# Routed feed-forward and attention steps: block-wise state signals, operation choice inside the feed, key table by operation, broadcast weight loads, drains on two engines

## What is computed

```
def step(h, p):
    op = jnp.argmax(h[0, 0, :NOPS])          # NOPS = 19
    q, k, v = h @ p['wq'][op], h @ p['wk'][op], h @ p['wv'][op]
    attn = softmax(einsum('bqd,bkd->bqk', q, k) * scale)
    y = einsum('bqk,bkd->bqd', attn, v) @ p['wo'][op]
    h = where(p['am'][op], y, h)
    z = relu(h @ p['w1'][op] + p['b1'][op]) @ p['w2'][op] + p['b2'][op]
    return where(p['fm'][op], z, h)
```

## Time and profile before

| | us |
|---|---|
| Executions timed | 602.72, 610.61, 612.91 |
| Median of the three | 610.61 |
| Profiled execution, its own time | 602.83 |
| Span in its profile | 600.8 |
| Granted TensorE clock over the span | 0.942 of full speed |

### The profile page before, as it was taken

One profiled execution on the slowest core, in us unless ns is written; L12 is line 12 of the kernel. 1 busy time (PEld: TensorE's weight loads), 2 busy tenths in 40 slices (PEclk: granted clock), 3 DMA queues, 4 the chain that ended last, 5 costly groups with the idle time before them and its releaser, 6 DMA issues.

```text
span 600.8 us, 10365 instructions
## 1 busy us (share of the span) xinstructions
PE 529.1 (88%) x3951; PEld 255.0 (42%) x3952; DVE 404.9 (67%) x740; ACT 318.4 (53%) x584; POOL 49.8 (8%) x106
## 2 busy tenths in 40 slices
PE   6999998998599989999999999999999652799962
PEld 5554654554133335444334443344444320366721
DVE  5655557357886746876887686876662556898662
ACT  2735445565256575556656566666656332655440
POOL 7031232113110000000000010000000000000000
PEclk9999999699679999999999999999999957999975
DMA  5000000000000000000000000000000000000001
GB/s 112 5 1 2 2 2 2 0 2 2 0 1 1 1 1 1 2 0 1 1 1 1 1 2 1 1 9 1 1 1 1 2 3 15 1 1 1 1 0 35
DMA packets 9511, 3.28 MB, mean 5 GB/s; under 512 B 8820, under 2 KB 9079, under 8 KB 9463
## 3 DMA queue, kind: packets, MB, share of 16 engines
q1 hardware_dynamic: 8182, 2.61, 1.9%
q10 hardware_dynamic: 1281, 0.01, 0.1%
HBM read 2.09 MB, written 0.52 MB: 4 GB/s over the span
## 4 chain that ended last, share of the span: by engine, by line
PE 76%; DVE 10%; issue 8%; ACT 3%; POOL 1%; POOLq 0%; DVEq 0%; ACTq 0%
PE PS L786 18%; PE PS L763 18%; PE PS L747 5%; PE PS L667 4%; PE PS L681 4%; PE PS L694 3%; PE PS L518 2%; PE PS L490 2%; PE PS L502 2%; PE PS L802 2%; PE PS L708 2%; PE PS L989 2%; PE PS L564 2%; DVE most L1550 2%; PE PS L582 1%
## 5 line engine op out<-in xcount | busy, mean ns | idle before, releaser
L1189 ACT ACTIVATE PT<-PS 128x512 f32<-128x512 f32 x256 | 138.7, 593 | 78.7 <-PE PS L763 78.3
L1550 DVE TENSOR_REDUCE most<-PS 128x2 f32<-128x1024 f32 x128 | 154.4, 1221 | 33.9 <-PE PS L747 33.0
L763 PE MATMUL PS<-qrow,aS 128*64 128x512 f16 x1024 | 134.5, 383 | 1.8 <-ACT PT L1189 1.8
L786 PE MATMUL PS<-PT,V 128*64 128x512 f32 x512 | 134.4, 604 | 0.0
L763 PEld LDWEIGHTS PS<-qrow,aS 128*64 128x64 f16 x1024 | 58.8, 110 | 68.8 <-issue 22.9
L1145 ACT ACTIVATE prob<-sbias,negm 128x320 f32<-128x320 f32 (+1 forms) x64 | 34.3, 537 | 44.1 <-DVE negm L1596 43.9
L747 PE MATMUL PS<-aS,qrow 64*128 64x512 f16 x256 | 41.6, 397 | 7.0 <-DVE most L1550 6.2
L786 PEld LDWEIGHTS PS<-PT,V 128*64 128x64 f32 x512 | 32.0, 136 | 37.0 <-ACT PT L1189 17.9
L667 PE MATMUL PS<-ident 128*128 128x256 f16 x128 | 39.1, 306 | 7.5 <-DVE negm L1596 6.3
L1307 POOL TENSOR_TENSOR rstd<-var,minus_half 128x8 f32<-128x8 f32 (+1 forms) x9 | 13.5, 1505 | 343.5 <-DVE var L1414 343.5
L339 DVE COPY PT<-PS 128x384 f32<-128x384 f32 (+1 forms) x32 | 16.7, 523 | 29.4 <-PE PS L694 29.3
(11 more groups left out here) (192 smaller groups left out, 657.2 us busy)
## 6 DMA issues: line engine op xcount, KB each, us to landing
xall<-in_x_dram SPq DMA_DIRECT2D x2, 256.0 KB, 4.4
out_dram<-x SPq DMA_DIRECT2D x4, 128.0 KB, 2.1
w<-in_L_attn_Wq_dram SPq DMA_DIRECT2D x2, 128.0 KB, 2.6
w<-in_L_attn_Wk_dram SPq DMA_DIRECT2D x2, 128.0 KB, 2.7
w<-in_L_attn_Wv_dram SPq DMA_DIRECT2D x2, 128.0 KB, 2.7
fc<-in_L_conv_fc_w_dram SPq DMA_DIRECT2D x2, 64.0 KB, 2.7
wu<-in_L_attn_Wu_dram SPq DMA_DIRECT2D x2, 64.0 KB, 2.3
w1s<-in_L_ffn_ffn_w_dram SPq DMA_DIRECT2D x2, 64.0 KB, 2.1
```

The source lines that it names most:

```text
L763: mm = pe.matmul(PS[h0:h0 + C, lane, :], aS[:, part, k0 + h0:k0 + h0 + C], qG[:, lane, toks], start=(part == 0), stop=(part == 1))
L786: mm = pe.matmul(PS[cols, 6 + g % 2, :], V[:, img * NT + kt, cols], PT[:, g % 2, lane, kt, :], start=(kt == 0), stop=(kt == NT - 1))
L1189: act.activation(PT[:, g % 2, lane, phase, :], PS[:, lane, :], ACT.Exp).then_inc(c1["exped"], 1)
L1550: dve.tensor_reduce(most[:, g % 2, u // 2, u % 2, :], PS[:, b0:b0 + 2, :], AX.X, ALU.max, negate=True)\
```

## The change

- **State by block.** One semaphore per block, `state_made[blk]`, counts how often the block has been written; the registers `nw` and `nb` hold that count now and at the update's begin. Every reader waits for its block's count alone. SP waits for blocks 1 and 3 (`state_read`) before it issues wo in an attention, and before w2s, b1s and b2s in a feed.
- **Order.** Blocks go in the order 0, 2, 1, 3 (`ORDER`), the routed pieces likewise.
- **Choice inside the feed.** PE does hidden 0 to 2, output 0, hidden 3, then `show_row` into bank 3 (`ROW`) as soon as block 0 is drained, then output 1. DVE does `choose` between its last hidden drain and its last output drain. Only an update without a feed chooses afterwards (`otherwise`, in an Else).
- **Key table.** Laid out operation by step; the key is 4 x (19 x step + operation) + flags less NONE, zero if dead, so one instruction and a contiguous reduction replace `keys_left`'s three; the table takes eight steps instead of seven. The word carries the operation: `choose` writes one number, and SP needs no `value_load`.
- **Weights.** ws, w1s and wo come by one DMA each that reads the source twice (128 rows), so that ACT and DVE split them with one instruction instead of two. ACT splits w1s ahead of the state.
- **Drains.** y of lane 0 is drained by ACT, lane 1 by DVE; the last y goes into OB. Feed outputs use banks 2 and 6.
- **Way out.** PE turns each block when its count is there, into banks 4, 5, 2, 3, without waiting for adds.

The core of the diff, with the lines that it adds and keeps; those that it takes out are in the listing above, except where a minus shows them. Indentation is cut by eight.

```diff
@@ scan
+        now_word = e.snap(word, min_val=0, max_val=4 * NOPS * NSTEP - 1)
         flags = e.snap(now_word % 4)
         e.reg_add(nu, nu, 1)
+        e.reg_mov(nb, nw)
         now = e.snap(nu, min_val=1, max_val=NSTEP)
+        with e.If(flags >= 2):
+            attend(e.snap(na, min_val=0, max_val=NSTEP - 1), written(), before(), now_word, now)
+            e.reg_add(na, na, 1)
+            e.reg_add(nw, nw, 1)
+        with e.If(e.snap(flags % 2) == 1):
+            feed(e.snap(nf, min_val=0, max_val=NSTEP - 1), written(), before(), now_word, now)
+            e.reg_add(nf, nf, 1)
+            e.reg_add(nw, nw, 1)
+        if otherwise:
+            with e.Else():
+                otherwise(written(), now)
...
@@ pieces
-ROUTED = [(what, lane, b) for what in ("k", "q") for lane in range(2) for b in range(NB)]
+ROUTED = [(what, lane, b) for what in ("k", "q") for b in range(NB) for lane in range(2)]
...
@@ PE, attend: y
+            if (g, lane) == (0, 0):
+                pe.wait_ge(wo_loaded, base(16) + 16)
+            elif (g, lane) != (1, 1):
+                pe.wait_ge(state_made[0 if g == 0 else 2], nw + 1)
...
@@ PE, feed to the end
+    def feed(nf, nw, nb, word, now):
+        bz, bs = pe.snap(nf * (B * NB)), pe.snap(nf * N_STATE)
+        def hidden_part(j):
+            pe.wait_ge(ffn_split, bs + (2 + j))
             pe.sem_inc(gate, 1)
+            toks = slice(ORDER[j] * BLK, (ORDER[j] + 1) * BLK)
             for half, filled in enumerate(("lo_filled", "hi_filled")):
                 for part in range(2):
+                    m = pe.matmul(PS[:, 2 * j + half, :], w1S[:, part, half * P:(half + 1) * P],
+                                  hS[:, toks], start=(part == 0), stop=(part == 1))
                 m.then_inc(rf[filled], 1)
+        def output_part(two):
+            pe.wait_ge(rf["lo_drained"], bz + 2 * (two + 1))
+            pe.wait_ge(rf["hi_drained"], bz + 2 * (two + 1))
             pe.sem_inc(gate, 1)
             for half in range(2):
                 for n in range(2):
+                    blk = ORDER[2 * two + n]
+                    m = pe.matmul(PS[n * C:(n + 1) * C, (2, 6)[two], :], w2s[:, half, :],
                                   Z[:, half, blk * BLK:(blk + 1) * BLK], start=(half == 0), stop=(half == 1))
             m.then_inc(ffn_out_filled, 1)
+        for j in range(3):
+            hidden_part(j)
+        output_part(0)
+        hidden_part(3)
+        pe.wait_ge(state_made[0], nw + 1)
         pe.sem_inc(gate, 1)
+        show_row()
+        output_part(1)
+    def otherwise(nw, now):
+        pe.wait_ge(state_made[0], nw)
+        pe.sem_inc(gate, 1)
+        show_row()
+    nw = scan(pe, attend, feed, otherwise)
+    for j, blk in enumerate(ORDER):
+        pe.wait_ge(state_made[blk], nw)
+        pe.sem_inc(gate, 1)
+        for k in range(QT):
+            t = blk * QT + k
+            m = pe.transpose(PS[:, (4, 5, 2, 3)[j], k * C:(k + 1) * C], aT[:, t * P:(t + 1) * P], ident[0:C, 0:C])
+        m.then_inc(end_filled, 1)
...
@@ ACT
+    def high_state(made, j, nw):
+        toks = slice(ORDER[j] * BLK, (ORDER[j] + 1) * BLK)
+        act.wait_ge(state_made[ORDER[j]], nw)
+        act.sem_inc(gate, 1)
+        act.activation(hS[0:C, toks], aT[:, toks], ACT.Copy).then_inc(made, 1)
+    def attend(na, nw, nb, word, now):
         base = lambda k: act.snap(na * k)
+        for j in range(2):
+            high_state(routed_high, j, nw)
         act.wait_ge(attn_loaded, base(48) + 48)
+        twice = ws[:, :, :].rearrange("c n (o d) -> c n o d", o=1).to_broadcast([P, 3, 2, C])
+        act.activation(wsS[:, 0], twice, ACT.Copy).then_inc(routed_high, 1)
+        for j in range(2, B * NB):
+            high_state(routed_high, j, nw)
         for n, piece in enumerate(ROUTED):
             act.wait_ge(routed_filled, base(len(ROUTED)) + (n + 1))
             high_part(piece, PS[:, n % 4, :], (1.0, C ** -0.5), routed_high)
+        def y_out(g):
+            act.wait_ge(c2["y_filled"], base(B * NB) + (2 * g + 1))
+            act.activation(aT[:, g * BLK:(g + 1) * BLK], y_bank(g, 0)[0:C, :], ACT.Copy)\
+               .then_inc(state_made[g], 1)
+        act_attention(act, c2, base, 2, y_out)
+    def feed(nf, nw, nb, word, now):
+        bz = act.snap(nf * (B * NB))
+        act.wait_ge(ffn_loaded, act.snap(nf * 64) + 64)
+        act.activation(w1S[:, 0], w1s[:, :], ACT.Copy).then_inc(ffn_high, 1)
+        for j in range(B * NB):
+            high_state(ffn_high, j, nw)
+        def drain_hidden(j):
+            toks = slice(ORDER[j] * BLK, (ORDER[j] + 1) * BLK)
+            act.wait_ge(rf["lo_filled"], bz + (j + 1))
+            act.activation(Z[:, 0, toks], PS[:, 2 * j, :], ACT.Relu, bias=b1s[:, 0:1],
                            scale=1.0).then_inc(rf["lo_drained"], 1)
+        def drain_output(two):
+            blk = ORDER[2 * two]
             act.wait_ge(ffn_out_filled, act.snap(nf * 2) + (two + 1))
+            act.activation(aT[:, blk * BLK:(blk + 1) * BLK], PS[0:C, (2, 6)[two], :], ACT.Identity,
+                           bias=b2s[0:C, 0:1], scale=1.0).then_inc(state_made[blk], 1)
+        for j in range(3):
+            drain_hidden(j)
+        drain_output(0)
+        drain_hidden(3)
+        drain_output(1)
...
@@ DVE, key table and choose
+    def keys_alive(chain, base):
+        dve.scalar_tensor_tensor(codew[:, :, :], by_op(steps[:, :]), nextf[:, 0:1], codes[:, :, :],
+                                 ALU.is_gt, ALU.mult).then_inc(chain, 1)
+    def keys_next(chain, base):
         dve.wait_ge(chain, base + 1)
+        dve.tensor_reduce(nextkey[:, :], codew[:, :, :], AX.X, ALU.min).then_inc(chain, 1)
...
@@ DVE, choose's end
-        dve.tensor_scalar(control[:, bass.ds(now, 1), 1:2], opf[:, :].rearrange("p (a b) -> p a b", a=1),
-                          64.0, None, ALU.mult)
-        dve.tensor_copy(control[:, bass.ds(now, 1), 0:1], nextf[:, :].rearrange("p (a b) -> p a b", a=1))\
-           .then_inc(control_ready, 1)
+        dve.tensor_scalar(control[:, bass.ds(now, 1), 0:1], nextf[:, :].rearrange("p (a b) -> p a b", a=1),
+                          float(NONE), None, ALU.add).then_inc(control_ready, 1)
...
@@ DVE, attend and feed
+    def low_state(high, done, count, j):
+        toks = slice(ORDER[j] * BLK, (ORDER[j] + 1) * BLK)
+        dve.wait_ge(high, count)
+        dve.tensor_tensor(hS[C:P, toks], aT[:, toks], hS[0:C, toks], ALU.subtract).then_inc(done, 1)
+    def attend(na, nw, nb, word, now):
         base = lambda k: dve.snap(na * k)
+        by, bp, bk = base(B * NB), base(N_SPLIT), base(NKEYS)
+        dve.wait_ge(control_ready, now)
+        keys_alive(attend_keys, bk)
+        keys_next(attend_keys, bk)
+        for j in range(2):
+            low_state(routed_high, routed_split, bp + (j + 1), j)
+        twice = ws[:, :, :].rearrange("c n (o d) -> c n o d", o=1).to_broadcast([P, 3, 2, C])
+        dve.wait_ge(routed_high, bp + 3)
+        dve.tensor_tensor(wsS[:, 1], twice, wsS[:, 0], ALU.subtract).then_inc(routed_split, 1)
+        for j in range(2, B * NB):
+            low_state(routed_high, routed_split, bp + (j + 2), j)
         for n, piece in enumerate(ROUTED):
+            dve.wait_ge(routed_high, bp + (N_STATE + n + 1))
             low_part(piece, PS[:, n % 4, :], (1.0, C ** -0.5), routed_split)
+        def y_out(g):
+            dve.wait_ge(c2["y_filled"], by + (2 * g + 2))
+            dve.tensor_copy(aT[:, TOK + g * BLK:TOK + (g + 1) * BLK], y_bank(g, 1)[0:C, :])\
+               .then_inc(state_made[NB + g], 1)
         dve_attention(dve, c2, base, 2, y_out)
+    def feed(nf, nw, nb, word, now):
+        bz, bs, bk = dve.snap(nf * (B * NB)), dve.snap(nf * N_STATE), dve.snap(nf * NKEYS)
+        dve.wait_ge(ffn_high, bs + 1)
+        dve.tensor_tensor(w1S[:, 1], w1s[:, :], w1S[:, 0], ALU.subtract).then_inc(ffn_split, 1)
+        for j in range(B * NB):
+            low_state(ffn_high, ffn_split, bs + (j + 2), j)
+        def drain_hidden(j):
+            toks = slice(ORDER[j] * BLK, (ORDER[j] + 1) * BLK)
+            dve.wait_ge(rf["hi_filled"], bz + (j + 1))
+            dve.tensor_scalar(Z[:, 1, toks], PS[:, 2 * j + 1, :], b1s[:, 1:2], 0.0,
                               ALU.add, ALU.max).then_inc(rf["hi_drained"], 1)
+        def drain_output(two):
+            blk = ORDER[2 * two + 1]
             dve.wait_ge(ffn_out_filled, dve.snap(nf * 2) + (two + 1))
+            dve.tensor_scalar(aT[:, blk * BLK:(blk + 1) * BLK], PS[C:P, (2, 6)[two], :], b2s[C:P, 0:1],
+                              None, ALU.add).then_inc(state_made[blk], 1)
+        drain_hidden(0)
+        dve.wait_ge(control_ready, now)
+        keys_alive(feed_keys, bk)
+        drain_hidden(1)
+        keys_next(feed_keys, bk)
+        drain_hidden(2)
+        drain_output(0)
+        drain_hidden(3)
+        dve.wait_ge(feed_keys, bk + NKEYS)
+        choose(now)
+        drain_output(1)
+    def otherwise(nw, now):
+        dve.wait_ge(attend_keys, 2)
```

(44 more changed lines are left out.)

250 lines of the change are left out of this document (67 added, 183 removed).

## The result

The changed kernel takes 598.32 us, the median of 20 runs (593.66 to 605.45), the kernel before on the same chip 604.20 (20 runs). The ratio is 0.9921, 95% interval 0.9896 to 0.9945: about 0.8% faster, less than the 2% at which this kernel is told from no change, and 0.2 us from the forecast. The ratio leaves out executions in a slower state (3 of the changed kernel's 20), so it is not the quotient of the two medians. The profiled execution takes 599.66 (span 597.8, clock 0.947); the one of before 602.83 (600.8, 0.942).

A forecast was written before the change was run, and what follows sets the result against it. PE was taken to bound the first 483.5 us, latency between engines the routed part outside the attention. Terms 1.2 - 3.75 - 1.1 - 2.7 - 0.1 = -6.45 from 602.83 gave 596.4; forecast placed at 598.5, range 592 to 606.5.

The forecast's parts named there:

- the placement: Forecast set at 598.5 us, between the terms' 596.4 and 604.2, the shown median less the gain of 6.45.
- Key table, 0: Eighth step of the key table, before 483.5 us: 0 added, hidden by PE; 0.8 if it displaced DVE.
- First feed's start, +1.2: SP's new wait for the state before three loads: first hidden matmul 1.2 us later, bounds 0 and +2.
- Inside a feed, word at H+10.05: Choosing beside the second output lands the control word 10.05 us after a feed's first hidden matmul (H); before 12.5, 12.8.
- First feed to attention, H+17.3: Attention's first matmul 17.3 us after the first feed's first hidden matmul (H), before 21.06: -3.75 us.
- The attention's end, -1.1: Parallel last drains and w1s's earlier single copy bring the second feed 1.1 us sooner; bounds -0.3 and -1.5.
- Way out, -2.7: Second control word to output transposes: same walk starts earlier, beside the second output, -2.7 us; bounds -1 and -3.3.
- Four banks, -0.1: Output transposes into four banks, four adds still following one another: -0.1 us, bounds +0.3 to -0.4.
- Rival 1: Clock stays at 1.2 GHz in the feeds as PE's stream is cut: +8.9, 605.3 us; chance 0.07.
- Rival 2: Sequencers' walks into the attention and out, and later SP loads, bind: 600.0 us; chance 0.2.
- Rival 3: Second feed runs at 2.4 GHz, hidden 0 to 2 faster: -2.0, 594.4 us; chance 0.13.
- a change ahead of 483 us: Sign of being wrong: any change before the routed part, where the edit was said to touch almost nothing.

## Why the prediction was right, and where it was not

The total came out near the sum: -6.45 forecast; 1.0 - 7.5 = -6.5 between events, -5.9 by the medians of the times and -4.8 by the ratio. But several terms are off, in both directions, and that they cancel to 0.1 is luck. So is the 0.2 us between 598.5 and the median: 2.1 us of the forecast are the placement above the sum's 596.4, which nothing in the sum gave; the sum alone is 1.9 us off the median.

- *Key table, 0.* **The step that failed**: +1.0, above the bound of 0.8. I counted one added instruction and did not price the casts, whose read changes from along to across, and I took PE's higher busy share (451 against 324 of 483.5) as cover. In this stretch about half of the added DVE time came through even so; whom it delays no run shows.
- *First feed's start, +1.2.* Measured +1.3 on the means (+1.4 in the profile shown). Mechanism shown: taking the wait away gives 1.0 to 1.6 back. H lay at D + 6.76 where I had 6.5; b2s took 2.9 us to be usable, not 2.2. That PE's walk would bind without the wait was right too.
- *Inside a feed, word at H+10.05.* Measured 9.2 to 10.2 in the first feed, 8.9 to 9.3 in the second, in three profiles. The order is as described and choosing behind the output again shows it to be the cause. Mis-sized was the clock: I had all of hidden 0 to 2 at 1.2 GHz. Where they were (first feed of the second of these profiles, where the run of twelve takes 5.28 us) the word came at H+10.20, so the rest of the sum is right to 0.15. In the first feed of the profile shown the clock rose during them, as its windows have it (columns as before):

```profile
493.80:495.80 2.00, 1.95 (x5) 0.73 (x6) 1.76 (x4) 1.43 (x3) 0.00 (x0) 0.50 0.00 0
495.80:497.80 2.00, 2.00 (x8) 0.73 (x6) 1.92 (x3) 0.71 (x2) 0.00 (x0) 0.69 0.00 0
497.80:499.80 2.00, 1.97 (x10) 0.57 (x8) 1.65 (x3) 0.66 (x1) 0.00 (x0) 1.00 0.00 0
```

- *First feed to attention, H+17.3.* Measured 9.32 + 8.08 = 17.4, from two errors: the word came 0.7 early and the weights 0.8 late. "Doubling ws by one broadcast DMA ... I give it nothing" is the mis-sized term: by the ranges above it delays the landing by 1.1 to 1.8 us against what two more instructions cost, a net loss of 0.4 to 0.6 on the mean. The sum looked at the time to issue, which stayed the same; what it lacked is how few DMA engines the load runs on.
- *The attention's end, -1.1.* -1.75. Of it the second drain engine is 0.2 and w1s's doubling 0.7; the rest, 0.85, lies in w1s's copy ahead of the state's and in the waits by block, which were not tried alone.
- *Way out, -2.7.* The start moved by H2-W2, -3.7 on the means, and the walk became 0.5 longer: -3.2, close to the bound of -3.3. *Four banks, -0.1:* T-E is 0.2 shorter.
- *Rival 1 (feeds stay at 1.2 GHz)* did not come. *Rival 2 (walks bind)* came in small part: PE's way out is longer by 0.5, and the last load of the first feed is there at D+4.96 where the sum had D+4.5. PE's way into the attention is not the bound (7.85 on the mean, 7.26 with the single load, where the rival had 8.6), and DVE's walk out is no longer than PE's. *Rival 3 (clock holds)* came in the profile shown: the window over the second feed stands at 1.00 and its x12 run takes 2.75 us. But it is worth only 0.4 (8.94 against 9.34 where the clock fell), not 2.0: by the rows DVE is then the bound, which no edit tested at this clock. Nor is it a gain in all: the two profiles in which the clock held have A-Y at 62.91 and 62.85, the nine others of changed kernels 61.66 to 62.13. The timeline there:

```profile
577.52 2.75 PE L1002 MATMUL PS<-aS,w1S 128*128 128x512 f16 x12 [2.17 <-DVE aS L1858]
...
579.88 0.85 DVE L1756 SCALAR_TENSOR_TENSOR codew<-steps,nextf,codes 1x627 f32<-1x627 f32 x1
580.65 0.73 DVE L1894 TENSOR_SCALAR PT<-PS,b1s 128x512 f32<-128x512 f32 x1
...
581.49 1.94 PE L1014 MATMUL PS<-PT,w2s 128*64 128x512 f32 x8 [1.22 <-issue]
```

The key work stands between hidden 0's and hidden 1's drains, and PE stands idle for 1.22 us until 0.1 us behind the end of the latter, at 581.38. The row gives "issue" and not DVE for this idle time; that it is this wait I conclude from the order in the program.

Of the signs named for being wrong one came, a change ahead of 483 us: the key table's 1.0. The attention was said to take 63 to 64 us from PE's first piece to its last y; from start to start it is 62.0 before and 62.2 after, unchanged as said, but read too long.

The placement between the profiled time and the median was no derivation. The series since put the kernel before at 603 to 606, except for its two repeats at 608 and 610, and the changed kernel at 597 to 599.

## What to carry to other kernels

Cut profiles at events and compare lengths between them: here 1.0 us in 195 repeats to 0.02 while the whole time moves by 6. When a layout is turned to make one instruction contiguous, price every instruction that fills it, and count an engine's added work as hidden only where a row shows who waits for it. Put the choice that starts the next stage, and the walk of the sequencers behind it, ahead of work that nobody waits for; halve instructions through a wider load only where that load is early, and look in the trace at how many DMA engines it keeps busy.
